# A wait in the middle of sixteen row gathers: GpSimd issues the second eight when the first eight have landed

## The reference

```python
h = x @ enc_node_w + enc_node_b
e = edge_attr @ enc_edge_w + enc_edge_b
for i in range(4):                       # the first without the norm and the residual
    z = relu(layernorm(h, ln_g[i], ln_b[i]))
    msg = relu(z[src] + e) + 1e-7        # one row of z for each edge
    alpha = segment_softmax(msg * t[i], dst)
    out = z + segment_sum(msg * alpha, dst)
    h = h + relu(layernorm(out @ w1[i] + b1[i])) @ w2[i] + b2[i]
```

## Time and profile before

| | |
|---|---|
| median of three runs | 4429.86 us |
| span of the profiled execution, first to last instruction | 4412.7 us |
| lies around it, by the median | 17.2 us |
| instructions | 44760 |
| PE, DVE, POOL, ACT busy | 66%, 64%, 57%, 39% of the span |
| mean granted TensorE clock | 0.771 |
| gathers of z rows (line 479) | 2488 |

### The profile page before, as it was taken

The page is one execution under the profiler, slowest core; times in us unless marked ns, Lnnn a source line. Parts: engine busy times, 40 slices in busy tenths (PEclk is TensorE's granted clock), DMA queues, the critical chain, the costliest instruction groups (busy, mean ns, idle before and its releaser), DMA issues.

```text
span 4412.7 us, 44760 instructions
## 1 busy us (share of the span) xinstructions
PE 2914.6 (66%) x16648; PEld 1382.9 (31%) x16648; DVE 2824.3 (64%) x2795; ACT 1741.2 (39%) x2192; POOL 2517.9 (57%) x2621
## 2 busy tenths in 40 slices
PE   3667677775437776777435777777742777777764
PEld 2223233332313333333222333333331333333333
DVE  6467678778436665666753666665763565666675
ACT  3356555545223333333432333333432333433343
POOL 6565656564366665666445666665627565655642
PEclk6778788877568888888656888887855787888875
DMA  6677778877237777777534777777734677777761
GB/s 153 162 219 204 215 195 222 219 198 174 59 100 204 204 204 192 204 204 204 133 81 115 204 204 204 205 205 201 191 76 104 160 199 199 204 202 190 211 153 40
DMA packets 1041338, 774.25 MB, mean 175 GB/s; under 512 B 914394, under 2 KB 935391, under 8 KB 1017504
## 3 DMA queue, kind: packets, MB, share of 16 engines
q1 hardware_dynamic: 934256, 446.17, 42.9%
q10 hardware_dynamic: 22048, 226.63, 14.0%
q0 software_dynamic: 84816, 98.59, 9.9%
HBM read 478.68 MB, written 292.44 MB: 175 GB/s over the span
## 4 chain that ended last, share of the span: by engine, by line
PE 41%; issue 23%; DVE 11%; ACT 10%; another core or an unknown queue 10%; POOL 4%; DMA 1%; SPq 0%; ACTq 0%; POOLq 0%; DVEq 0%
PE X L537 32%; PE X L520 5%; POOL gath L479 4%; DVE decay L885 3%; PE X L547 2%; DVE state_all L916 2%; ACT msg L647 2%; DVE X L890 1%; ACT shared L676 1%; ACT X L649 1%; ACT decay L659 1%; ACT X L664 1%; DVE state_all L900 1%; ACT decay L637 1%
## 5 line engine op out<-in xcount | busy, mean ns | idle before, releaser
L479 POOL DMA_INDIRECT gath<-z_table,idx x2488 | 2396.0, 963 | 1606.0 <-issue 750.5
L537 PE MATMUL X<-one_hot,z_parts 128*64 128x512 fp8e5 x13800 | 2103.0, 427 | 840.8 <-issue 773.1
L537 PEld LDWEIGHTS X<-one_hot,z_parts 128*64 128x64 bf16 x13800 | 939.4, 120 | 2071.2 <-issue 1542.8
L883 DVE TENSOR_TENSOR decay<-decay,top 128x1 f32<-128x1 f32 x216 | 34.2, 158 | 1358.5 <-ACT X L649 1179.6
L647 ACT ACTIVATE msg<-X,edge_bias 128x1024 f32<-128x1024 f32 (+2 forms) x216 | 228.2, 1057 | 1622.5 <-remote 1080.3
L520 PE MATMUL X<-attr,enc_edge 128*128 128x512 f32 x824 | 469.3, 688 | 221.9 <-issue 115.8
L659 ACT ACTIVATE decay<-X 128x1024 f32<-128x1024 f32 (+2 forms) x216 | 209.3, 969 | 791.7 <-DVE X L890 556.1
L871 DVE STREAM_TRANSPOSE rows_all<-state_all 128x1024 f32<-128x1024 f32 (+3 forms) x432 | 505.9, 1171 | 7.5
L885 DVE TENSOR_TENSOR_SCAN decay<-X,decay 128x1023 f32<-128x1023 f32 (+2 forms) x216 | 477.2, 2209 | 7.7
L900 DVE TENSOR_TENSOR_SCAN state_all<-decay,state_all,X 128x1024 f32<-128x1024 f32 (+2 forms) x216 | 468.2, 2167 | 20.0 <-ACT X L664 16.0
L916 DVE TENSOR_TENSOR_SCAN state_all<-decay,state_all,X 128x1024 f32<-128x1024 f32 (+2 forms) x216 | 468.0, 2167 | 0.0
(11 more groups left out here) (155 smaller groups left out, 1182.3 us busy)
## 6 DMA issues: line engine op xcount, KB each, us to landing
rows_table<-rows_all SPq DMA_DIRECT2D x784, 256.0 KB
one_hot<-one_hot_dram ACTq DMA_DIRECT2D x69, 1920.0 KB
attr<-attr_t SPq DMA_DIRECT2D x196, 512.0 KB
one_hot<-one_hot_dram ACTq DMA_DIRECT2D x69, 1280.0 KB
one_hot_dram<-one_hot SPq DMA_DIRECT2D x23, 1920.0 KB
gath<-z_table,idx POOLq DMA_INDIRECT x2488
one_hot_dram<-one_hot SPq DMA_DIRECT2D x23, 1280.0 KB
keep<-keep_dram SPq DMA_DIRECT2D x192, 128.0 KB
```

Of the source, the lines that this page charges most:

```text
L479: pool.indirect_dma_start(out=gath[s][:, n * F:(n + 1) * F], out_offset=None, in_=z_table, in_offset=bass.IndirectOffsetOnAxis(ap=idx[:, c ...
L537: last = nc.tensor.matmul(x[h * F:(h + 1) * F, BANK:CH], z_parts[:, i * GB + k, third, :], one_hot[:, i, k, h * BANK:(h + 1) * BANK], star ...
```

## The change

In a chunk that is gathered whole (`gathered_tiles(layer, c) == KT`, eight tiles, sixteen gathers) POOL waits, before it issues the ninth gather, until the first eight have landed. `before` is the number of gathers that this slot's semaphore has counted in the chunks before. It applies to chunks 0 to 3 and the odd ones from 5 to 47, 26 chunks in each of 4 layers, 104 waits. In chunk 0, which has no first tile, six gathers stand before the wait and eight behind it.

```diff
@@ -475,6 +475,9 @@
                         pool.wait_ge(x_ready, g - SLOTS + 1)
                     settle()
                     for n in range(first_tile(c) * HALVES, gathered_tiles(layer, c) * HALVES):
+                        if n == KT and gathered_tiles(layer, c) == KT:
+                            before = GATHERS_UP_TO[g - SLOTS] if g >= SLOTS else 0
+                            pool.wait_ge(gathered[s], 16 * (before + KT - first_tile(c) * HALVES))
                         col = STARTS[c] // P * HALVES + n
                         pool.indirect_dma_start(out=gath[s][:, n * F:(n + 1) * F], out_offset=None, in_=z_table,
                                                 in_offset=bass.IndirectOffsetOnAxis(ap=idx[:, col:col + 1], axis=0))\
```

## The result

| | before | changed | ratio, 95% interval |
|---|---|---|---|
| median of the runs | 4434.78 us (5 runs) | 4796.09 us (5 runs) | 1.0805 [1.0764, 1.0846] |
| span of the profiled execution | 4412.7 us | 4756.0 us | |

The change costs 8%. The forecast was 4350 us, in a range that ended at 4490: wrong in sign and outside the range.

A forecast was written before the change was run, and what follows sets the result against it. It took PE's signals, held back while POOL gathers back to back, to set the period. Savings of 32, 31 and 19 us made -82 on a 4412.7 us span: 4331, plus 17.2 around it 4348, stated as 4350; range 4250 to 4490.

The forecast's parts named there:

- What bounds the kernel now: Layers 1 to 3, 37.24 us period: PE's signals are held back while POOL gathers back to back, released in its pauses.
- Step 1: POOL's first run: first gather at 0.81 us, then one every 1.248, so the eighth starts at 9.55.
- Step 2: The added wait: eighth to ninth gather start takes 2.9 to 4.8 us, taken as 4.2; 307 us if nothing came back.
- Step 3: Odd chunk released at 12.2 us instead of 23.4; PE's 90 matmuls then run freely, through by 25.4.
- Step 4: Layers 1 to 3: a run of sixteen follows, even chunk released at 36.33; period 36.7 us, 32 us less.
- Steps 5 and 6: Layer 0: chunks 7 to 25 at 40.1 us a period, 31 less; chunks 27 to 47 at 37.5, 19 less.
- Step 7: Start of each layer: five waits, 14.8 us, covered by POOL's own stand of 16.30 before chunk 6; counted 0.
- Step 8: The wait as an instruction, the semaphore and the tail of a layer: 0.
- Nothing is released in the wait: Rival, pause between eighth and ninth gather: odd chunk still released after the sixteenth; 4663 to 4700 us; chance 0.10.
- The wait is long: Rival: a one-hot load and row stores delay the eighth gather's landing; pause 6.0 us gives 4490; chance 0.12.

The follow-up runs named there:

- wait after twelve: Changed kernel with its wait after the twelfth gather instead of the eighth: 4527.08 us, 1.0176; 3988.58 us, 1.1172 where the kernel before takes 3568.01.
- third group: Runs on one chip where the kernel before took 4449.48 us: changed kernel again (4786.94 us, 1.0752) and three variants of where it waits.
- both waits: Changed kernel plus a second wait, after the sixteenth gather: 4366.75 us, 0.9915; on two other chips 1.2706 and 1.2736.
- first group: Four runs on one chip where the kernel before took 4403.83 us; there the wait in layer 0 alone took 4346.16 us, 0.9856.
- a met wait: Kernel before, with a wait at the change's place whose value was reached three chunks ago, so POOL runs through: 4401.3 us, 1.0007.
- wait after four: Changed kernel with its wait after the fourth gather instead of the eighth: 3767.53 us, 1.057, where the kernel before takes 3566.0.

## Why the prediction was wrong

**What bounds the kernel now:** the reading held where it was made. Signals and matmuls of PE are held back in POOL's runs on the chips on which the kernel before takes 4404 to 4449 us. Moving the pauses moves the stretches in which PE is slow with them. On the three other chips neither happens, with the same instructions, so it is no property of the kernel alone, which one trace could not show. Nor do the traces show by what way a run of gathers holds PE back.

**Step 1** held: the eighth gather 8.75 us after the first.

**Step 2** took the wrong end. I put 4.2 us between eighth and ninth gather and measured 2.65 (median 2.69), below my own low end of 2.9. I had chosen the loaded value because a one-hot load would be under way, but in the period shown none is: it is issued at 1598.35, behind the pause. The Trainium skill, DMA: Bandwidth & Descriptors, section "Anatomy of one DMA — SWDGE (gpsimd) path", gives about 2.0 us plus bytes / 436e3. For 32 KB, and with the 0.4 for the resumption, that is an estimate of 2.5, and this trace agrees with it (2.65). On the quicker chips the pause is 7.00 in the chunk shown and 6.8 on average, beyond both, with the load ahead of the gather.

**Step 3** is the one that failed. Its first half held in part: the odd chunk is released earlier (18.2 us behind the even one; forecast 12 to 13, before 23.4), though only 3.0 and 6.1 us behind the ninth gather (1598.35, 1601.44); the pause is no longer than the 2.6 to 2.7 us that signals had needed. Its second half said that PE's 90 matmuls "run freely" and "are through by 25.4", because the ninth gather "starts a fresh run". They were through at 1626.57, which in the forecast's count of time (0 is the even chunk's load, 1582.61) is 44.0. A pause of 2.65 us did not start a fresh run: PE thinned out 3 us behind the ninth gather and was nearly stopped 8.2 us behind it. A pause of 4.43 us did free it (wait after twelve: 71 matmuls in one piece).

The changed kernel shows the same within one execution, since a few of its pauses were longer. POOL and PE in such a place of layer 1:

```profile
1897.73 0.94 POOL L482 DMA_INDIRECT gath<-z_table,idx  x1 [0.30 <-issue]
1901.61 0.94 POOL L482 DMA_INDIRECT gath<-z_table,idx  x1 [2.93 <-DMA gath<-z_table,idx]
...
1920.32 0.94 POOL L482 DMA_INDIRECT gath<-z_table,idx  x1 [0.30 <-issue]
1926.14 0.94 POOL L482 DMA_INDIRECT gath<-z_table,idx  x1 [4.88 <-PE X L550]
```

```profile
1900.37 8.79 PE L540 MATMUL X<-one_hot,z_parts 128*64 128x512 fp8e5 x79 [0.41 <-issue]
```

With a pause of 3.88 us PE does 79 of the 90 in one piece, beside the same run of sixteen, and POOL then stands 5.82 us and not 13.86. In layers 1 to 3 the wait's run of eight is followed by a run of sixteen 63 times. After 56 pauses of 2.60 to 2.77 us POOL's stand at the end of that run is 8.0 to 14.5 us, 13.3 in the median; after four of 3.05 to 3.22 it is 7.3 to 11.0; after three of 3.63 to 4.12 it is 5.3 to 7.0. The two other profiles with these waits on a chip of the slower kind (third group) have the same: 8.3 to 14.8 us after pauses of 2.5 to 2.8, and 5.0 to 6.7 after those of 3.5 and more. No edit set these lengths, but kernel, chip and execution are the same for all of them. So the step failed on the length of the pause. In the rows shown PE gets going again 1.67, 1.72, 2.69 and 3.65 us after the start of a run's last gather; a pause of 2.65 ends within that range, but that this is the reason is not shown.

**Step 4** saw what came next and priced it wrong. It says that the eight gathers follow without a pause and make one run of sixteen, and then has the even chunk turned at 26 and released at 36.33. The run came, PE was held back in it, and release came when PE was through, at 44.0. The rows for this stood in the prediction: the run of 24 after an early release, with 56 matmuls left. I used them only against a rival, and did not give the period its length. And even by its own numbers the step had little to win: it set 36.7 against a mean of 37.24, while the cycle of the earlier trace rows took 35.7. In the kernel before, POOL's first gathers behind the even chunk on both sides of it:

```profile
3016.35 0.94 POOL L479 DMA_INDIRECT gath<-z_table,idx  x1 [2.33 <-remote]
...
3059.74 0.94 POOL L479 DMA_INDIRECT gath<-z_table,idx  x1 [13.73 <-PE X L547]
```

It took 43.4 us, with POOL idle for 13.73 us behind PE at its end. There are three such runs of 24 in the 60 steady periods of layers 1 to 3. The new cycle is this long period made the rule: 42.7 us is the mean now, with 12.9 idle. Kernels that keep the early release and bring a long enough pause back show it from the other side: after twelve 1.0176, both waits 0.9915.

**Steps 5 and 6:** not in the changed kernel (42.2 and 39.8 us a period for 40.1 and 37.5), but in the kernel with the wait in layer 0 alone on the chip of the first group (39.3 and 37.0). On that of the third group layer 0 gained nothing: 4786.94 us with it, 4788.31 without. Why the same code finds two rhythms stays open.

**Step 7** held roughly: from the end of one layer's window to the start of the next it was 334.0, 325.6 and 322.7 us and is 328.4, 326.2 and 334.5, in sum 6.9 us more against a forecast of none. **Step 8** held; a met wait costs nothing.

**The rivals.** *Nothing is released in the wait* had the sign and, at 4663 to 4700, was nearest, but for another reason: the release did come early, and waiting cost little in itself. *The wait is long* has its place on the quicker chips: pause 7.00 us, 1.16. On those chips every wait was paid, and two of them cost 1.27. The Trainium skill, DMA: Bandwidth & Descriptors, section "Rules for kernel authors", has the rule for this, issue early and wait late, and those traces agree with it. On the slower kind it does not decide, since two waits took 0.9915 there. A rival was missing: that the early release removes the pause behind the sixteenth gather, and PE's window with it. The trace of before could have priced it: 43.4 us a period in place of 37.24 is 60 x 6.2 = 370 us, 4800.

**What stays open.** Why chips differ, and by what way a run of gathers holds back PE and its signals. How long a pause must be: of the lengths seen, those up to 2.8 us left nearly the whole loss, those around 3.1 a part, and those from 3.5 on little, but no run set the length by itself. Both waits and the changed kernel were never timed on one chip of the slower kind, so 0.9915 beside 1.0752 compares ratios of two chips; wait after twelve beside the changed kernel does not have that gap. And the wait after four was not seen on such a chip.

## What to carry to other kernels

When a change releases something early, ask which wait now falls away behind it, and what used that wait as its window: here 8% was lost because the pause that was added, 2.65 us, was too short to replace the one that vanished, 4.70 us. A rare pattern in the trace of before (3 long periods in 60) is the forecast for a change that makes its condition the rule; price it before setting it aside. And a schedule that lives on pauses has to be timed on more than one chip: two waits were worth 0.9915 on one and 1.27 on two others.

## What the runs showed that I had not expected

The same program takes 4404 to 4449 us on some chips and 3566 to 3568 on others. What the profiles show of the difference is the idle time ahead of the one-hot matmuls, 1114.1 us against 20.3 in the changed kernel, and their busy time, 2176.4 against 1535.6. The mean granted clock of that kernel is 0.747 of full speed in the one profile and 0.776 in the other: 4% apart, where the busy time of these matmuls is 42% more, so it is not the cause by itself. The order of kernels turns over with it: with both waits the kernel takes 4367 us on a chip of the slower kind and 4531 and 4541 on the quicker ones.
